# An attention layer with a quantised FFN on one core: fourteen blocks of VectorE in head 0, value products ahead of the upper keys' lengths, and ten norms on GpSimd

## The reference

```
ct_q = x Wd_q + b;  query = heads(ct_q Wu_q + b) + heads(rope(ct_q Wq_r + b))
ct_kv = x Wd_kv + b; key  = heads(ct_kv Wu_k + b) + heads(rope(x Wk_r + b))
value = heads(ct_kv Wu_v + b)
x = layernorm(x + softmax(query key^T / sqrt(272)) value Wo + b)
x8 = clip(round(x / s)), s = max(|x|) / 127 over the whole array
x = layernorm(x + (x8 W8^T) * s * weight_scale + bias)
```

## Time and profile before

| | us |
|---|---|
| median of 3 runs (lowest, highest) | 1922.75 (1921.45, 1923.99) |
| the profiled execution, its span | 1922.54, 1920.7 |
| first exponential starts, last ends | 122.25, 1842.2 |
| busy: TensorE, ScalarE, VectorE, GpSimd | 1840.5, 1804.4, 1583.1, 178.4 |
| TensorE's last value product ends; last evacuation ends | 119.8, 120.5 |
| VectorE's last step on the last query chunk ends | 125.0 |
| GpSimd's 32 additions of the output bias | 166.8 to 221.0 |
| TensorE's last FFN product ends | 1905.2 |
| first batch's inverse ready; ScalarE's first norm of the tail starts | 1898.6, 1900.9 |
| ScalarE's last norm ends | 1914.9 |

### The profile page before, as it was taken

One profiled execution on the slowest core, in us unless ns is written; L12 is line 12 of the kernel. 1 busy time (PEld: TensorE's weight loads), 2 busy tenths in 40 slices (PEclk: granted clock), 3 DMA queues, 4 the chain that ended last, 5 costly groups with the idle time before them and its releaser, 6 DMA issues.

```text
span 1920.7 us, 31434 instructions
## 1 busy us (share of the span) xinstructions
PE 1840.5 (96%) x12988; PEld 446.8 (23%) x12988; DVE 1583.1 (82%) x1502; ACT 1804.4 (94%) x2024; POOL 178.4 (9%) x132
## 2 busy tenths in 40 slices
PE   8989999999999999999999999999999999999965
PEld 3442222221221222222122222222222212221235
DVE  3868979988888887888888888888888888988577
ACT  3479999999999999999999999999999999999956
POOL 5645600000000000000000000000001000500010
PEclk9999999999999999999999999999999999999987
DMA  4534111111111011111121101111121101111012
GB/s 142 167 128 151 20 18 23 26 26 26 26 26 25 17 20 19 23 26 26 25 70 26 26 14 19 20 26 25 26 48 26 25 16 20 17 26 26 1 25 88
DMA packets 161383, 73.41 MB, mean 38 GB/s; under 512 B 129968, under 2 KB 146608, under 8 KB 160752
## 3 DMA queue, kind: packets, MB, share of 16 engines
q1 hardware_dynamic: 158224, 66.79, 15.1%
q10 hardware_dynamic: 3008, 4.53, 0.8%
HBM read 49.13 MB, written 20.84 MB: 36 GB/s over the span
## 4 chain that ended last, share of the span: by engine, by line
ACT 53%; PE 30%; issue 8%; DVE 7%; DMA 1%; POOL 0%; ACTq 0%; DVEq 0%; SPq 0%; POOLq 0%
ACT arena L909 52%; PE PS L708 14%; PE PS L658 9%; PE PS L1196 4%; DVE arena L969 2%; PE PS L749 1%; DVE arena L945 1%; DVE arena L955 1%; PE PS L1344 1%; ACT arena L869 0%; PE PS L1169 0%; DVE bn L837 0%; DVE arena L953 0%; DVE arena L965 0%; DMA arena<-arena 0%
## 5 line engine op out<-in xcount | busy, mean ns | idle before, releaser
L909 ACT ACTIVATE arena<-PS 128x1024 f32<-128x1024 f32 x1860 | 1709.7, 1278 | 10.4 <-PE PS L658 8.5
L708 PE MATMUL PS<-arena,Vh 128*32 128x512 f32 x8192 | 1091.5, 605 | 8.9 <-DVE arena L945 8.9
L658 PE MATMUL PS<-Qst,Kst 49*128 49x512 f16 x4096 | 717.5, 383 | 26.9 <-issue 4.6
L969 DVE SCALAR_TENSOR_TENSOR arena<-arena 128x2048 f32<-128x2048 f32 x282 | 645.5, 2289 | 0.1
L945 DVE TENSOR_SCALAR arena<-PS 128x512 int32<-128x512 f32 x376 | 259.5, 690 | 240.0 <-PE PS L658 235.5
L658 PEld LDWEIGHTS PS<-Qst,Kst 49*128 49x128 f16 x4096 | 183.6, 93 | 1030.6 <-ACT arena L909 982.9
L708 PEld LDWEIGHTS PS<-arena,Vh 128*32 128x32 f32 x8192 | 161.7, 108 | 328.5 <-issue 326.5
L965 DVE SCALAR_TENSOR_TENSOR arena<-arena 128x2048 f32<-128x2048 f32 x94 | 216.5, 2303 | 0.0
L953 DVE TENSOR_SCALAR arena<-arena 128x2048 int32<-128x2048 int32 x94 | 116.9, 1244 | 8.2
L955 DVE TENSOR_SCALAR arena<-arena 128x2048 int32<-128x2048 int32 x94 | 117.9, 1254 | 0.0
L1519 POOL TENSOR_SCALAR nmr<-mv 128x16 f32<-128x16 f32 x1 | 0.3, 263 | 1258.3 <-DVE mv L1698 1258.3
(11 more groups left out here) (120 smaller groups left out, 479.9 us busy)
## 6 DMA issues: line engine op xcount, KB each, us to landing
Qst<-q_halves SPq DMA_DIRECT2D x64, 128.0 KB
Kst<-k_halves SPq DMA_DIRECT2D x64, 128.0 KB
Vh<-head_values SPq DMA_DIRECT2D x30, 256.0 KB, 5.5
k_halves<-parts_or_sums SPq DMA_DIRECT2D x16, 256.0 KB, 3.1
q_halves<-parts_or_sums SPq DMA_DIRECT2D x16, 256.0 KB, 2.6
Qst<-q_halves SPq DMA_DIRECT2D x64, 64.0 KB
Kst<-k_halves SPq DMA_DIRECT2D x64, 64.0 KB
head_values<-arena SPq DMA_DIRECT2D x1, 4096.0 KB, 14.3
```

The source lines that it names most:

```text
L658: return nc.tensor.matmul(out, Kst[par][low:low + HK + 1, at:at + 128], Qst[par][low:low + HK + 1, j * CH:(j + 1) * CH], start=True, stop= ...
L708: last = nc.tensor.matmul(bank(value_bank(t))[32 * j:32 * j + 32, :], Vh[t % 2][:, kt, :], moving, start=kt == first, stop=kt == last_kt)
L909: nc.scalar.activation(ring(at, k), bank(g % SLOTS * SLOT, k), ACT.Exp, scale=EXP_SCALE).then_inc(a.exp, 1)
L969: last = nc.vector.scalar_tensor_tensor(out=t, in0=t, scalar=POLY[3 - j], in1=power if j == 3 else mantissa, op0=ALU.add, op1=ALU.mult)
```

## The change

The attention's order gets 14 blocks instead of 13 for head 0, which shifts the number of every later block by one. Three of the 16 value products move in front of the lengths of the upper keys; the turned maximum's column and ScalarE's first shift stand at value product 10 now, the table of the exponential is loaded right behind the shift. VectorE's step on the upper keys' lengths, row and column move forward, and so does `first_sums`, which waits for `bias_out`. C of queries and C of keys swap places, so ring groups 4 to 7 wait one by one for the late queries' parts. Scores of the first three groups wait each for their own banks and stand in front of `bias_out`. The FFN weights' six operations are spread over six hooks. In the tail, tiles 0 to 5 and 12 to 15 are normed by GpSimd instead of ScalarE, the first batch's inverse comes two rounds later, and SyncE's stores wait for the new counts.

```diff
@@ -59,7 +59,7 @@
 LAG = 4
 VALUE_PHASES = (0, 1, 2)
 BLOCK_PHASES = (2, 1)
-FIRST_BLOCKS, FIRST_BLOCK = 13, 11
+FIRST_BLOCKS, FIRST_BLOCK = 14, 11
 LENGTHS_STEP = 8
 BEFORE = 3
 BEHIND = 4
@@ -195,14 +195,19 @@
 K_GROUPS, Q_GROUPS = (DKV, KR_, UK_, KHI), (DQ_, QR_, UQ_, QHI)
 
 
+EARLY_VALUES = 3
+
+
 def make_products():
 
     order = [("p", c, e) for c in range(HALF_CH) for e in range(8)]
     for c in range(HALF_CH, NCH):
         order += [("p", c, e) for e in (DKV, KR_, DQ_, UK_, KHI)]
     for c in LATE:
+        if c == LATE[2]:
+            order += [("v", 0, n) for n in range(EARLY_VALUES)]
         order += [("p", c, QR_), ("p", c, UQ_), ("p", c, QHI)]
-    return order + [("v", 0, n) for n in range(KT // 2)]
+    return order + [("v", 0, n) for n in range(EARLY_VALUES, KT // 2)]
 
 
 PRODUCTS = make_products()
@@ -392,7 +397,7 @@
         K1 = 1024
 
 
-        C = {n: [cut((2 * m + p) * K1, (2, CH)) for p in range(2)] for m, n in enumerate("kq")}
+        C = {n: [cut((2 * m + p) * K1, (2, CH)) for p in range(2)] for m, n in enumerate("qk")}
         A = {n: [cut(4 * K1 + (2 * m + p) * CH, (CH,)) for p in range(2)] for m, n in enumerate("kq")}
         B = {n: [cut(6 * K1 + (2 * m + p) * CH, (CH,))[0:TURNED, :] for p in range(2)] for m, n in enumerate("kq")}
         tab = [cut((8 + p) * K1, (2, CH))[0:TURNED, :, :] for p in range(2)]
@@ -525,6 +530,7 @@
         e_rs2 = sem("inverse_deviations2")
         e_fa = sem("out_by_scalar")
         e_fv = sem("out_by_vector")
+        e_fp = sem("out_by_gpsimd")
         e_out = sem("stored")
 
         class Attention:
@@ -717,9 +723,11 @@
                 pe.wait_ge(b_bits, QB * (CYCLE_OF[n] + 1))
                 project_tile(n, bank(project_bank(n))[:, 0:D]).then_inc(p_proj, 1)
 
+            for g in range(SLOTS):
+                pe.wait_ge(s_ev, max(DONE[p] for p in PRODUCTS if PRODUCT_BANK[p] // SLOT == g))
+                scores(g)
+            pe.wait_ge(s_ev, len(PRODUCTS))
             bias_out()
-            for g in range(SLOTS):
-                scores(g)
             for s in range(STEPS_ALL + 1):
                 if s == LENGTHS_STEP:
                     half_1_lengths()
@@ -864,6 +872,11 @@
                 nc.vector.tensor_scalar(Y[:, t, :], Y[:, t, :], rstd[:, t:t + 1], nmr[:, t:t + 1],
                                         ALU.mult, ALU.add).then_inc(s, 1)
 
+        def norm_by_gpsimd(tiles):
+            for t in tiles:
+                nc.gpsimd.tensor_scalar(Y[:, t, :], Y[:, t, :], rstd[:, t:t + 1], nmr[:, t:t + 1],
+                                        ALU.mult, ALU.add).then_inc(e_fp, 1)
+
         def norm_by_scalar(s, tiles):
             for t in tiles:
                 nc.scalar.activation(Y[:, t, :], Y[:, t, :], ACT.Identity, bias=nmr[:, t:t + 1],
@@ -901,11 +914,12 @@
                 k, at = len(blocks), (RING_FIRST + g * SLOT) % RING
                 if g == 0:
 
+
                     act.wait_ge(s_rope, ROTATED[LATE[1], "q"])
                 if g == 2:
                     act.wait_ge(s_rope, ROTATED[PARTS[-1]])
-                if g == 4:
-                    act.wait_ge(s_dve, len(STEP))
+                if 4 <= g < 8:
+                    act.wait_ge(s_dve, STEP["low", LATE[g - 4], "q"])
                 nc.scalar.activation(ring(at, k), bank(g % SLOTS * SLOT, k),
                                      ACT.Exp, scale=EXP_SCALE).then_inc(a.exp, 1)
 
@@ -1142,13 +1156,17 @@
                 sp.dma_start(out_d[first * 128:end * 128, :].rearrange("(t p) n -> p t n", p=128),
                              Y[:, first:end, :]).then_inc(e_out, 16)
 
-            for first, end in ((0, 4), (4, 8), (8, 12), (12, 17)):
-                store(e_fa, end, first, end)
-            store(e_fa, 22, 17, 22)
+            store(e_fp, 4, 0, 4)
+            sp.wait_ge(e_fp, 6)
+            store(e_fa, 2, 4, 8)
+            store(e_fa, 6, 8, 12)
+            sp.wait_ge(e_fp, 10)
+            store(e_fa, 7, 12, 17)
+            store(e_fa, 12, 17, 22)
             store(e_fv, 3, 22, 25)
-            store(e_fa, 25, 25, 28)
+            store(e_fa, 15, 25, 28)
             store(e_fv, 6, 28, 31)
-            store(e_fa, 26, 31, KT)
+            store(e_fa, 16, 31, KT)
             sp.wait_ge(e_out, 16 * 9)
 
         @block_.tensor
@@ -1225,7 +1243,7 @@
                     pe.wait_ge(s_ev, in_bank(SMALL_BANK))
                     pe.wait_ge(s_kmax, 3)
                     nc.tensor.transpose(PS[0:1, SMALL_BANK * CH:SMALL_BANK * CH + 128], kmax[:, 2:3], ident[:, :]).then_inc(s_kt, 1)
-                if p == ("v", 0, 8):
+                if p == ("v", 0, 10):
                     pe.wait_ge(s_kmax, 5)
                     nc.tensor.matmul(PS[:, SMALL_BANK * CH + 128:SMALL_BANK * CH + 129], kmax_row[0:1, 32:160], ones[0:1, 0:1],
                                      start=True, stop=True).then_inc(s_kt, 1)
@@ -1233,7 +1251,6 @@
 
             pe.wait_ge(s_shift, 1)
             pe.wait_ge(s_range, 1)
-            pe.wait_ge(s_ev, len(PRODUCTS))
             pe.wait_ge(s_rows_in, 64)
 
             attention_tensor(pe, fast, lambda: lengths("q", 1, Q_LENGTH_BANKS[1]))
@@ -1410,9 +1427,9 @@
                 evacuate(p)
                 if p[0] == "p" and p[2] == KHI and p[1] + 2 < NCH:
                     load_x(act, p[1] + 2)
-                if p == ("v", 0, 7):
+                if p == ("v", 0, 10):
                     first_shifts()
-            nc.scalar.activation(xs[:, 0:1], small[:, 6:7], ACT.Exp)
+                    nc.scalar.activation(xs[:, 0:1], small[:, 6:7], ACT.Exp)
 
             attention_scalar(act, fast)
 
@@ -1458,15 +1475,14 @@
 
 
             act.wait_ge(e_rs2, 2)
-            norm_by_scalar(e_fa, range(0, 6))
+            norm_by_scalar(e_fa, range(6, 12))
             act.wait_ge(e_mv2, 22)
             deviation(e_sd2, *BATCHES2[1])
-            norm_by_scalar(e_fa, range(6, 12))
             act.wait_ge(e_rs2, 4)
-            norm_by_scalar(e_fa, range(12, 16))
+            norm_by_scalar(e_fa, range(16, 20))
             act.wait_ge(e_mv2, 28)
             deviation(e_sd2, *BATCHES2[2])
-            norm_by_scalar(e_fa, range(16, 22))
+            norm_by_scalar(e_fa, range(20, 22))
             act.wait_ge(e_mv2, KT)
             deviation(e_sd2, *BATCHES2[3])
             act.wait_ge(e_rs2, 6)
@@ -1544,6 +1560,10 @@
             add_ffn_bias(e_zb, 1, 12, 16)
             pool.wait_ge(e_fin, 12)
             add_ffn_bias(e_zb, 1, 6, 12)
+            pool.wait_ge(e_rs2, 2)
+            norm_by_gpsimd(range(0, 6))
+            pool.wait_ge(e_rs2, 4)
+            norm_by_gpsimd(range(12, 16))
 
 
         @block_.vector
@@ -1628,6 +1648,12 @@
                 dve.wait_ge(s_shift, 1)
                 nc.vector.reduce_max(kmax[:, 4:5], bank(Q_LENGTH_BANKS[0]), AX).then_inc(s_range, 1)
 
+            def first_sums():
+
+                nc.vector.memset(sums_ok[:, :], 1.0).then_inc(s_sums, 1)
+                dve.wait_ge(s_bo, 1)
+                nc.vector.tensor_tensor(bo, PS[:, OT * CH:OT * CH + D], bo, ALU.add).then_inc(s_bo2, 1)
+
             def half_1_shifts():
 
                 dve.wait_ge(s_len, 4)
@@ -1646,18 +1672,16 @@
                 vector_step(name, c, n)
                 if (name, n) == ("low", "k") and c == HALF_CH + 2:
                     key_lengths(0)
+                if (name, c, n) == ("low", NCH - 1, "k"):
+                    key_lengths(1)
                 if (name, c, n) == ("low", LATE[0], "q"):
-                    key_lengths(1)
-                if (name, c, n) == ("add", LATE[1], "q"):
                     key_row()
                 if (name, c, n) == ("high", LATE[1], "q"):
                     key_column()
                 if (name, c, n) == ("low", LATE[1], "q"):
                     query_lengths()
-            nc.vector.memset(sums_ok[:, :], 1.0).then_inc(s_sums, 1)
-
-            dve.wait_ge(s_bo, 1)
-            nc.vector.tensor_tensor(bo, PS[:, OT * CH:OT * CH + D], bo, ALU.add).then_inc(s_bo2, 1)
+                if (name, c, n) == ("low", LATE[2], "q"):
+                    first_sums()
             half_1_shifts()
 
             def check_range():
@@ -1679,15 +1703,17 @@
                                             ALU.mult).then_inc(s_range, 1)
                 dve.wait_ge(s_range, 12)
 
-            def ffn_weights():
-
-                nc.vector.tensor_tensor(wscaled, w8[:, :, :], fs2, ALU.mult).then_inc(s_wp, 1)
-                for n in range(3):
-                    dve.wait_ge(s_wp, 2 * n + 1)
+            def ffn_weights(step):
+
+                n, rest_of = divmod(step - 1, 2)
+                if step == 0:
+                    nc.vector.tensor_tensor(wscaled, w8[:, :, :], fs2, ALU.mult).then_inc(s_wp, 1)
+                    return
+                dve.wait_ge(s_wp, step)
+                if rest_of:
+                    nc.vector.tensor_tensor(wscaled, wscaled, wparts[n], ALU.subtract).then_inc(s_wp, 1)
+                else:
```

(8 more changed lines are left out.)

## The result

The changed kernel takes 1905.72 us (median of four runs, 1904.75 to 1905.90), the kernel before 1923.37 in the same series (1921.45 to 1926.77): ratio 0.9900, 95% interval 0.9883 to 0.9916. By the medians that is -17.65 us (by the ratio, which isn't their plain quotient of 0.9908, -19.2), where -8.7 was forecast and the range ended at 1909. The direction was right, the forecast half of the measured size.

What follows compares the result with a forecast made beforehand. The prediction took ScalarE's exponentials, 1709.7 of 1920.7 us, as the bound. Its terms -2.7 - 2.8 - 1.4 + 1.9 - 3.7 summed to -8.7 us, so 1914.0 us, with a range of 1909 to 1920.

Steps and rivals of the forecast that it cites:

- Start: Ahead of the first exponential: it starts at 119.5 us instead of 122.25, -2.7 us.
- the filled wait: At the start: three value products fill TensorE's 2.41 us idle before the key lengths, which then run at full clock.
- SyncE's chain: At the start: from ScalarE's shift to the landed shift rows, 2.8 + 0.8 + about 1.8 us, ahead of the first score.
- Rival (a): At the start: TensorE's clock drops after idling from 116.0 to 119 us, 0.4 + 1.0 us more, 1915.4; chance 0.12.
- Borders: Between heads: shifted block numbers remove nine ScalarE gaps of 0.29 us and one of 0.20, -2.8 us.
- Projected tiles: Behind projected tiles: two pairs of 1.13 + 0.29 us gaps instead of three, -1.4 us.
- the step rule: At projected tiles: 3 steps to the next block, at 2, 8 and 14 before, at 5 and 11 after, bring gap pairs.
- Heads 0 and 1: First heads: the fourteenth block and GpSimd's additions delay VectorE by 2.0 us in all, net +1.9 us.
- Theory A: Experiments' expectation: gaps cost added distance between exponentials' starts, not counted idle time; borders 4.7 us, projected tiles 5.4.
- Weights: Near 352 us: six operations lie inside 160 us without a gap, so spreading them over six hooks is worth 0.
- Tail: After the last exponential: GpSimd's norms at 0.50 us and earlier stores end the span at 1917.0 us, -3.7 us.
- break-even: In the tail: at 1.08 us per GpSimd norm the span would end at 1920.7 us, as before.

Runs made afterwards that it cites:

- e10: Changed kernel with no value product ahead of the last two query chunks' products, all sixteen behind; 1907.29 us, ratio 0.9912 to the kernel before.
- e1: Kernel before with fourteen blocks instead of thirteen in head 0 and nothing else of the change; 1915.95 us, ratio 0.9961.
- e4: Kernel before with the value product at projected tiles 2, 8 and 14 moved two steps earlier, ahead of the projection; 1919.64 us, ratio 0.9978.
- e5: Changed kernel with the value product at projected tiles 5 and 11 put back to the next block's step; 1910.07 us, ratio 0.9926 to the kernel before.
- e7: Changed kernel with GpSimd's 32 additions of bias and x paced, one behind each 25 exponentials from number 125; 1905.49 us, ratio 0.9900 to the kernel before.
- e9: Changed kernel with thirteen blocks in head 0 again, all else as changed; 1916.68 us, ratio 0.9963 to the kernel before.
- e6: Changed kernel with the weights' six VectorE operations again at one hook, block 50; 1907.91 us, ratio 0.9915 to the kernel before.
- e11: Changed kernel with bias_out again ahead of the first three groups of scores; 1907.76 us, ratio 0.9915 to the kernel before.
- e12: Changed kernel with each of GpSimd's ten norms done twice, first into a spare buffer; 1910.50 us, ratio 0.9931 to the kernel before.
- e3: Kernel before with only the tail's edits: GpSimd's ten norms, first inverse two rounds later, new store order; 1920.11 us, ratio 0.9982.
- e8: Changed kernel with the old ring wait, group 4 waiting for all of VectorE's early steps; 1909.94 us, ratio 0.9927 to the kernel before.

## Why the prediction was wrong, step by step

- **Start, -2.7.** Right: -2.83 in the pair, and over all profiles 107.97 to 109.25 with the old start (five) against 105.07 to 106.15 with the new (nine). Of the reason given, e10 shows that the gain goes when the three products stand behind, and doesn't tell the filled wait from the fewer products ahead of the column; that SyncE's chain comes last is shown by the 2.71 us in front of the scores. Rival (a), a clock drop, happened, and cost the changed kernel less than its 1.4 us: one exponential was 0.26 us late.
- **Borders, -2.8.** The mechanism was right (every border's gap went, in e1 too), the term mis-sized: -4.7. The price of a gap was its counted 0.29 or 0.20; by distances a border gives back 0.63 and 0.30. Only seven of the nine gaps of 0.29 stood at borders, so the counted term should have been -2.2; the other two, behind tiles 4 and 10, went as well.
- **Projected tiles, -1.4.** This is the step that failed, together with the price of a gap: pairs of gaps were to come wherever "the block behind a projected tile follows the tile's last block by 3 steps". The 3 steps came at tiles 5 and 11, as worked out from the step rule, and no pair did. e4 and e5 show what the rule left out: whether a value product stands ahead of the wait, worth 1.10 us a tile. All three pairs went, and by distances the term is -5.4.
- **Heads 0 and 1, +1.9.** GpSimd's additions and the fourteenth block are the cause (e7, e9), at the two places forecast, but VectorE was late by less: head 1 took +1.12, about 0.8 of it by the fourteenth block. Head 0's -0.90 isn't the change's own but luck of the execution: with the same blocks and ring e5, e6, e10 and e11 have 1.59 to 1.78, e7 1.07 and e12 3.11. These go with where and how long TensorE ran at half speed; no run tests that alone.
- **Where the body's 7.6 us came from.** In counted idle time the body was to lose 2.3 us. The gaps that the timelines list fell by 7.35: the three pairs 4.26 (1.4 expected), the nine of 0.29 and the 0.20 2.8, as expected, the gap of 0.93, against three of 0.29 in place of the 0.23 (+0.64, where +1.9 was expected). So 2.8 us of the miss are the pairs, 1.3 head 1, 0.9 head 0, and the other 2.5 are lost overlap that the counted time doesn't hold. Theory A laid all on the counting; it is a third.
- **Weights, 0.** Wrong by 0.54 (head 4 of e6 and of e1): work covered "in 160 us without a gap" was covered for the old block number.
- **Tail, -3.7.** Right: -3.64, the norm (0.54 us for 0.50) and the break-even too (e3, e12).
- **The rule against the norms' move.** By the Trainium skill, GPSIMD Engine Reference, 4.1 Engine selection, elementwise work belongs on VectorE, and GpSimd takes about twice as long for two inputs and is near line rate for one. A norm reads one tensor, so the 0.80 us that the prediction priced was the other case's. Measured, a record lasts 0.56 us against 0.41 on VectorE (1.4 times) and 0.59 on ScalarE, and norms start 0.54, 0.33 and 0.49 us apart; the trace lies between the page's two cases. Since the stores wait for ScalarE's norms there and VectorE is busy, the move pays all the same (e3).

Alone the parts give -7.5, -3.1 and -3.5, -14.1 in all (each within 2 to 3 us). By the profiles the change is -2.9 (start, the median of nine against that of five), -9.0 (body, e11 against e9) and -3.9 (rest, the median of nine against that of four), -15.8. The measured -17.65 lies 2 above; its interval (-22.5 to -16.2) nearly reaches it. In the profiled pair the surplus is mostly the 1.45 us to the 13th matmul and the 0.9 in head 0. Whether the timed runs had the same luck isn't shown.

## What to carry to other kernels

Size a stall of the bounding engine by the distance between starts, summed and held against the usual distance, not by counted idle time: here overlapping records hid 0.63 of the 0.92 us at a border and 0.63 of the 2.05 us of a pair. Where one number shifts a whole schedule, read each place's order of jobs in the new table, not one rule for all: a single job moved ahead of a wait was worth 1.1 us each time. Work is covered at a place, not in general; move the place and price it again.

## What was unexpected on the chip

- The first 12 matmul records take 6.80 to 8.47 us between executions of the same instructions, and everything behind them shifts with it.
- TensorE ran at the lower of its two levels, a granted clock of 0.50, once in every execution between 118 and 136 us: for 3.4 us in eight, 6.8 in four (e1, e5, e6, e9) and 10.2 in two (e8, e12). Head 0's excess over the usual distances lies between 0.70 and 3.11 us for the same start and blocks. A stretch at 97 us came in four of the five executions with the old start (not in e3) and in none of nine with the new.
- A GpSimd norm of 256 columns with two scalars per partition starts 0.54 us behind the one before it (a record lasts 0.56), for ten in the changed kernel and for most of e12's twenty in a row, beside VectorE's and ScalarE's tail work.
